# Loading 4-bit weights from another queue and naming the activation table once: one layer (attention, LoRA FFN) on eight cores

## The reference

```python
xn = _layernorm(x, axis=-1)                       # x: (1, 16384, 4096)
# attention: "sequence" is the head dimension of one token
q = einsum('bse,edh->bsdh', xn, Wq) + bq          # 32 heads of 128
k, v = ...                                        # 8 heads of 128, repeated 4 times
scores = einsum('bsdh,bseh->bsde', q, k) / sqrt(128)      # 128 x 128 for each token
attn = softmax(scores, axis=-1)
a = einsum('bsde,bseh->bsdh', attn, v).reshape(..., 4096)
# ffn: W = nibbles(qweight) * scale + zero, 4096 x 4096, plus a rank-16 LoRA
f = einsum('bsi,oi->bso', xn, W) + 2 * (xn @ lora_A.T) @ lora_B.T
out = x + a + f
```

## Time and profile before

| what | us |
|---|---|
| median of 2 runs | 7076.39 |
| the two runs | 7044.18, 7108.6 |
| profiled execution | 7035.2 |
| its span, slowest core (core 2) | 7033.1 |
| spans of all eight cores | 6999.4 to 7033.1 |
| mean granted TensorE clock of core 2 | 0.687 |
| busy: PE, DVE, ACT, POOL | 3768.2, 1353.8, 1229.8, 136.9 |

### The profile page before, as it was taken

The page is one execution under the profiler, slowest core; times in us unless marked ns, Lnnn a source line. Parts: engine busy times, 40 slices in busy tenths (PEclk is TensorE's granted clock), DMA queues, the critical chain, the costliest instruction groups (busy, mean ns, idle before and its releaser), DMA issues.

```text
span 7033.1 us, 53749 instructions; the slowest of 8 cores (6999.4 to 7033.1 us)
## 1 busy us (share of the span) xinstructions
PE 3768.2 (54%) x17384; PEld 1604.5 (23%) x17600; DVE 1353.8 (19%) x2259; ACT 1229.8 (17%) x1664; POOL 136.9 (2%) x262
## 2 busy tenths in 40 slices
PE   0666655554256665454426775555452666555454
PEld 0222222121122222221112222221121222222121
DVE  3000122222300012222230002222223000222222
ACT  2000122221300012221230001221223000222221
POOL 0000000000000000000000000000000000000000
PEclk9888755676578865577657786556665788555667
DMA  2566300222222200022222220012221222001222
GB/s 69 146 166 171 79 6 18 87 81 84 99 72 84 96 25 6 23 86 80 95 84 84 84 85 24 6 35 78 99 84 73 95 84 87 12 6 37 98 87 79
DMA packets 154908, 508.57 MB, mean 72 GB/s; under 512 B 68100, under 2 KB 68308, under 8 KB 105494
## 3 DMA queue, kind: packets, MB, share of 16 engines
q1 hardware_dynamic: 93160, 265.31, 10.5%
q0 software_dynamic: 33456, 210.44, 10.3%
q10 hardware_dynamic: 28032, 29.39, 1.2%
HBM read 458.34 MB, written 84.03 MB: 77 GB/s over the span
## 4 chain that ended last, share of the span: by engine, by line
PE 42%; DMA 19%; DVE 14%; ACT 12%; issue 8%; ACTq 4%; SPq 1%; DVEq 0%; POOLq 0%
PE pf L463 12%; PE pAB L463 9%; ACT wring L851 6%; PE pf L880 6%; PE pAB L880 6%; DMA wring<-wbq 4%; DVE Mb L618 4%; ACTq L567 4%; DMA qtb<-qt 3%; PE pAB L676 3%; ACT Et L720 3%; PE pV L693 2%; DMA wring<-wq 2%; DVE dqs L832 2%; DVE dqs L829 2%
## 5 line engine op out<-in xcount | busy, mean ns | idle before, releaser
L463 PE MATMUL pf<-wring,xnT 128*128 128x512 bf16 x3008 | 872.9, 458 | 707.4 <-DMA wring<-wbq 318.5
L880 PE MATMUL pf<-wring,xnT 128*128 128x512 bf16 x2004 | 705.5, 513 | 794.4 <-ACT wring L851 792.5
L463 PE MATMUL pAB<-wring,xnT 128*128 128x512 bf16 x3008 | 675.4, 379 | 3.3
L720 ACT ACT_TABLE_LOAD x64 | 82.1, 1283 | 3376.2 <-PE pAB L676 3376.2
L463 PEld LDWEIGHTS pf<-wring,xnT 128*128 128x128 bf16 x3072 | 342.5, 114 | 1235.9 <-issue 1013.9
L851 ACT ACTIVATE wring<-dqs 128x2048 bf16<-128x2048 int32 x256 | 488.8, 1909 | 585.8 <-DVE dqs L829 234.2
L880 PEld LDWEIGHTS pf<-wring,xnT 128*128 128x128 bf16 x2048 | 229.5, 120 | 1264.8 <-issue 1179.3
L599 PE MATMUL pAB<-k_sh,qg_sh 8*128 8x128 bf16 x2048 | 317.6, 284 | 349.5 <-DMA k_sh<-k_rm 326.6
L676 PE MATMUL pAB<-qg_sh,k_sh 9*128 9x128 bf16 x2048 | 370.4, 286 | 191.3 <-DMA qg_sh<-Mt_s 171.8
L880 PE MATMUL pAB<-wring,xnT 128*128 128x512 bf16 x2004 | 450.2, 379 | 2.3
L720 ACT ACTIVATE Et<-pAB 128x256 bf16<-128x256 f32 x1024 | 385.0, 383 | 260.9 <-PE pV L693 203.8
(11 more groups left out here) (93 smaller groups left out, 1491.9 us busy)
## 6 DMA issues: line engine op xcount, KB each, us to landing
qtb<-qt SPq DMA_DIRECT2D x128, 1024.0 KB, 5.0
wring<-wbq POOLq DMA_DIRECT2D x96, 1024.0 KB, 6.4
wring<-wq POOLq DMA_DIRECT2D x32, 1024.0 KB, 9.3
xt<-xin SPq DMA_DIRECT2D x16, 2048.0 KB, 7.9
xr<-xin SPq DMA_DIRECT2D x128, 256.0 KB, 5.6
out<-cmbU SPq DMA_DIRECT2D x128, 256.0 KB, 2.0
wring<-wbk POOLq DMA_DIRECT2D x24, 1024.0 KB, 6.6
wring<-wbv POOLq DMA_DIRECT2D x24, 1024.0 KB, 6.0
```

The costliest lines, as they stand in the source:

```text
L463: ins = e.matmul(banks[m], xnT_ap(k, m), wring[:, slot * 512:(slot + 1) * 512], start=(jj == 0 and half == 0 and k == half * 16), stop=False)
L720: i2 = e.activation(dst, src, AF.Exp, scale=INVSQ)
L880: ins = e.matmul(banks4[m], xnT_ap(k, m), wring[:, slot * 512:(slot + 1) * 512], start=(k == 0), stop=(k == 31))
```

## The change

```diff
@@ -151,6 +151,9 @@
         for s_ in sem.values():
             nc.sync.sem_clear(s_.h)
         nc.all_engine_barrier()
+        nc.scalar.add_instruction(mybir.InstLoadActFuncSet(
+            name=nc.get_next_instruction_name(),
+            act_func_set_id=6, ins=[], outs=[]))
 
         blk = ctx.enter_context(nc.Block())
 
@@ -792,9 +795,6 @@
                     e.dma_start(out=bzr[:, (nb % 2) * 512:(nb % 2 + 1) * 512],
                                 in_=bz_dram[:, nb * 512:(nb + 1) * 512]).then_inc(sem["bzl"].h, 16)
                     sem["bzl"].v += 16
-                blk.gpsimd(ffn_gp)
-
-                def ffn_xr(e, c=c, nb=nb):
                     dqx0 = sem["dqx"].v
                     for h in range(4):
                         tgt = dqx0 + 2 * h - 2
@@ -804,6 +804,9 @@
                         e.dma_start(out=qtb[:, (h % 2) * 2048:(h % 2 + 1) * 2048],
                                     in_=src).then_inc(sem["qtl"].h, 16)
                         sem["qtl"].v += 16
+                blk.gpsimd(ffn_gp)
+
+                def ffn_xr(e, c=c, nb=nb):
                     nbg = c * FNB + nb
                     if nbg >= 1:
                         e.wait_ge(sem["cmb"].h, 4 * nbg)
```

## The result

The changed kernel took 6666.67 us in the median of 12 runs (6590.66 to 6784.46), beside 7083.0 us for the kernel before (7038.0 to 7187.81, 10 runs). Forecast were 6610 us against 7040, 0.939, and a range of 6560 to 6785. In some executions one die runs one to three per cent longer at a lower granted clock, and the median of 6667 holds milder ones of these, which is why it lies above the forecast while the ratio does not.

The account below looks back on a forecast made before the run. The prediction took hand-overs, with PE waiting on DMA, DVE and ACT, to bound the kernel. Its terms, 265.1 + 82.1 + 41.1 + 41.1 = 429.4 us, subtracted from 7039.7 gave 6610 us, range 6560 to 6785.

Parts of the forecast that it names:

- The 28 waits between blocks, 265.1 us: FFN: DVE's waits for qtb between blocks of a chunk vanish with the loads on POOL; 265.1 us gained.
- The mid-block loads: FFN: the 32 qtb waits inside blocks grow by 1.4 us each, covered by 4.49 us free; 0 booked.
- waits for `qtb` of over 6 us in mid-block: FFN: sign of being wrong, meant to show POOL's second-half loads coming late; the limit was 6 us.
- rival 4: FFN: POOL's second-half loads land late and eat the gains, up to 7429 us in all; chance 0.04.
- The compiler leaves out its own loads: Whole program: one explicit table load makes the compiler drop its 144; the 128 on the path are worth 164 us.
- Rival 1: Whole program: all 144 compiler-placed table loads stay despite the explicit one, 6774 us; chance 0.15.
- Attention, 82.1 us: Attention: 64 table loads ahead of each batch's first exp go, 1.283 us each; 82.1 us gained.
- Rival 2: Attention: PE sets a batch's pace, so the table loads were covered and 82 us are not gained, 6692 us; chance 0.06.
- Layer norm, 41.1 us: Layer norm, lines 318 and 336: 32 table loads between ACT and DVE hand-overs go; 41.1 us gained.
- nothing for line 303: Layer norm, line 303: 16 table loads hidden behind DVE's reduction by 1.25 us; 0 booked, 20.5 us the bound.
- FFN loads, 41.1 us: FFN: 32 table loads between the unpack and the first conversion go; 41.1 us gained.
- The clock pays it back: FFN dense matmuls: shorter pauses lower the granted clock to 0.82, costing 69 us, 6679 us; chance 0.05, opposite 0.02.

Follow-up runs that it names:

- e1: Changed kernel without the explicit table load, so only the qtb loads moved to POOL; ratio 0.9531 to the kernel before, slowest span 6754.5 us.
- e3: Changed kernel with the qtb loads back on SP, the next block's first two ahead of this block's stores; ratio 0.9361 to the kernel before.
- e4: Changed kernel with qtb piece 2 waiting for the fourth unpack, as piece 3 does; FFN stage sum 2059 us in a single execution.
- e4b: Changed kernel with a 2 MB load into the idle xt issued ahead of qtb piece 3; FFN stage sum 2120 us in a single execution.
- e2: Kernel before plus only the explicit table load, qtb loads still on SP; ratio 0.9649 to the kernel before, slowest span 6865.5 us.
- e6: Changed kernel with one table load per attention batch ahead of ACT's first wait; attention 1652 and 1654 us, against 1651 in the changed kernel.
- e5: Changed kernel with four table loads ahead of the first Square of each layer norm tile; layer norm sum 575 and 579 us, against 532.

## Why the prediction was right, point by point

- **What bounds the kernel.** Right. Of the 17.75 us of PE's pause in the earlier trace rows the DMA wait (10.38) and the table load (1.28) went and 6.01 are left, so nothing else moved into the gap.
- **The 28 waits between blocks, 265.1 us.** Right in place, small in size: 274 us in e1. The waits are gone, and DVE's timeline has the unpack right behind the combine. e3 shows the cause as the prediction has it, the place behind the stores, not the queue's engine. Of the 9 us more, 5.5 stand in PE's `pf` matmuls (714.8 us in e1, 720.3 before, core 5 of both); the rest is within the scatter of the sums. One reading of the prediction is wrong without harm: h=1 does not go in the first half of block nb-1. The eighth unpack follows the sixth conversion, which waits for the end of that half; on core 5 of the changed kernel PE ends it at 1290.0, the eighth unpack starts at 1294.61 and POOL issues the load at 1296.39. It still lands more than 20 us before DVE's last combine.
- **The mid-block loads, 1.4 us later and covered.** Right that they are covered, too large in size and wrong in kind. The row of the weight loads stood for a longer landing; what grew is the wait, by 0.8 us in the mean of the cores, and POOL's part of it, about 0.5 us, lies before the issue. The sign "waits for `qtb` of over 6 us in mid-block" came true (mean 6.1, core 1 6.5) and did not mean what the prediction made of it: its own figures, 5.07 + 1.4, pass that mark, and so it could not tell rival 4 from the forecast. The mark is where the cover ends, at a wait of some 10 us by e4 and e4b; the longest single wait of the changed kernel's core 1 is 8.0.
- **The compiler leaves out its own loads.** Right, in e2 as well as in the changed kernel: the explicit load stands ahead of all blocks, and none is placed in any later block. Rival 1 falls. The Trainium skill (ScalarE activation tables, "Table sets in the compiler and the runtime") has the loads placed per block; the counts before agree, and the count of one after shows that a program's own load ahead of the blocks can end this. This was the least certain step, and it was an assumption: no row of before could have told it. Why the compiler stops stays open: no run has an explicit load of a set that lacks a function used later, or one that stands in a later block alone.
- **Attention, 82.1 us.** Right: 85. Rival 2 falls by e2, and e6 shows from the other side that the load's cost was its place behind the wait.
- **Layer norm, 41.1 us, and nothing for line 303.** Right: 42 us (40 in e2). e5 measures the cover of line 303 without a load: four loads of 5.15 us make DVE wait 2.7 us, so it is some 2.4 us, where the rows of before gave 1.25 + 1.28 = 2.5.
- **FFN loads, 41.1 us.** Right in place; alone they bring 53 to 60, of which 15 are matmuls that run at the higher clock level. With the queue already changed they bring 36 (2091 in e1, 2055 in the changed kernel). So the two gains do not add up: 274 and 53 to 60 would be 327 to 334, and the whole change has 311, where 306 were forecast. In `pf` the two edits alone gain 5.5 and 15 us and both together 11 (709.5 us, core 5), which is 9 of the 16 to 23 us; the rest is not traced. That the sum comes so near the forecast is in part luck: it holds gains that were booked at nothing.
- **The clock pays it back.** Not seen. Over the last 11.7 us of each half, the stretch of the earlier trace rows, core 5 has a mean granted clock of 0.889 before and 0.896 after; 0.82 would have been the loss. The mean over the whole span rose on die 1 from 0.686 to 0.704, and the QKV sum is the same within 2 us. Neither the loss of 69 us nor the gain of 70 came; the 11 us in `pf` are a small piece of the latter.
- **The number.** 429.4 us were booked, and the stage sums give 42 + 85 + 311 - 1 = 437. The lowest run is 6590.66 us, the medians are 416 us apart.

## What to carry to other kernels

A DMA's place behind stores in a queue cost its whole latency in every round here, some 9 to 12 us of waiting; look for a load whose issue follows the last store of the round before, and put it where only its own buffer's release holds it. The same instruction cost its full time behind a wait and nothing ahead of it, so what an instruction on a mostly idle engine costs is read from its place in the order, not from the engine's busy share. After a gap is closed, the next serial pair shows its price at once: here moving four unpacks was worth 260 us, six tenths of what the whole change had brought. And a sign of being wrong has to lie where the cost begins: here that was the end of the cover, not the first growth of the wait.

## What was not expected of the hardware

Where a pause was shorter by 1.3 to 10 us, some of the dense matmuls behind it were faster too: their mean fell from 515 to 506 ns (e2) and 508 ns (changed kernel, core 5), at an unchanged 379 ns for the `pAB` groups. By the count of matmuls at the higher level it is 868 of 2048 before, 901 in e1, 947 in e2 and 920 in the changed kernel. It is 5 to 15 us in all, and why e1 with the larger cut got the smaller part of it (512 ns) stays open.
